# The first layer of a four-layer transformer kernel with another order of its pieces, written out as a table

## The chip, the cores and the metric

The kernel runs on one core of a Trainium2 chip. A core has five engines with instruction streams of their own, which meet only at semaphores: TensorE (PE, matrix products and transposes through the array), VectorE (DVE), ScalarE (ACT), GpSimd (POOL) and SyncE (SP, which only issues transfers here). The metric is the device time of one execution in microseconds, the median of several runs.

## The reference

Four layers, each a cross attention over 77 context rows per batch and then a feed-forward part. `x` has 4 x 512 = 2048 rows of 128 numbers. Only the first layer is touched:

```python
x = x + _L0_xattn_ref(_layernorm(x, axis=-1), ctx_1024, ctx_1024, mask_1x1xSxS2_fk1, ...)
x = x + _L0_ffn_ref(_layernorm(x, axis=-1), L0_ffn_gate_w, L0_ffn_w_up, L0_ffn_w_down, L0_ffn_expert_bias)
...
# _L0_xattn_ref, 16 heads of 8
q = _split_heads(query @ Wq + bq)
k = _split_heads(key @ Wk + bk)
v = _split_heads(value @ Wv + bv)
scores = jnp.einsum('bhqd,bhkd->bhqk', q, k) * scale
scores = scores + mask * -1000000000.0
attn = jax.nn.softmax(scores, axis=-1)
x = jnp.einsum('bhqk,bhkd->bhqd', attn, v)
return x.transpose(0, 2, 1, 3).reshape(...) @ Wo + bo
...
# _L0_ffn_ref, 8 experts, the best 2 for each row
scores = jax.nn.sigmoid(xf @ gate_w.T)
_, sel = jax.lax.top_k(scores + expert_bias, TOP_K)
# for each expert: (square(relu((xf * weight) @ wu.T))) @ wd.T, added up
```

## The kernel before

The 2048 rows are 16 tiles of 128. Work is cut into pieces such as `("S", 0, 3, 1)`, in the text S.0.3.1: kind S, layer 0, tile 3, second half of the heads. `make_plan` writes one list of pieces, the plan. Each engine's program walks that list and emits, for each piece, the instructions it has in it; so one list sets the order on all five engines, and the engines run apart from it only where no semaphore holds them.

The kinds of the first layer, with the line of their instructions in the profile of before:

- ln.q.0.g.0 to 7: the row normalisation of query group g, in steps (statistics L1385 and L1402 on DVE, step 2 on ACT L1889 and L1892, then L1406, L1410, L1415, and the scaled rows in steps 6 and 7, L1429, on DVE). ln.r is the same for the rows that go to the experts.
- xt: these rows turned by PE (L1073), and copied out by ACT (L1917). wq: the query projection (PE L1083), copied out half by DVE (L1323) and half by ACT (L1929), with the bias. The query groups are tiles 0, 1 to 3, 4 to 7, 8 to 11 and 12 to 15, and S of a tile waits for its group's wq.
- a0.n: the keys of batch n spread over heads (DVE L1344, four multiplications). vbd.n: the values likewise, on POOL (L2102, 2 instructions); vw0.n.q: turned by PE (L1023) and copied by ACT (L1852). xb: a bias on POOL (L2123).
- S: scores of a tile and 8 heads (PE L1095, 2 products recorded as 4). max: their maxima (DVE L1453). exp: the exponentials, 8 instructions on ACT (L1939). T.0.i.q: the probabilities turned by PE (L1118), in three parts q. copy.0.i.q: T copied out of its bank, by ACT (L1974) for q = 0 and 1 and by DVE (L1331) for q = 2. O: probabilities times values, and the sums (PE L1134, L1138). div: DVE L1495, L1499. Wo: PE L1151. add: DVE L1511. stat: DVE L1375.
- route.0.g.k and weigh: the choice of two experts for row group g and the place of each row in its expert's list, many short DVE instructions (L1521 to L1610) with PE products at k = 0 (L1163) and k = 9 (L1172 to L1176). send.0.i.c: an indirect DMA by POOL (L2143) that puts tile i's rows in place; 32 of them in the layer, in bursts of 8, 8, 6, 6 and 4.
- half, prod (PE L1037) and even, fold: work on the keys of layer 1, laid between.

Banks of the product memory bind the pieces: PE writes T with q = 0 and 2 to bank 4, and T with q = 1, xt and wq to bank 5, and a bank has to be copied out before its next writer. S of one half of the heads has banks 0 and 1, of the other 2 and 3, and they are free after that half's exp.

```python
bank_t = {p: 5 - (p[0] == "T" and p[3] != 1) for p in plan if p[0] == "wq" or p[0] == "T" and p[1] == 0 or
          p[0] == "xt" and p[2] == 0}
```

The expert blocks (X, U, H, D) start when all rows are sent, in `first`. Before, the plan of layer 0 came from rules: `first_order` for a tile's pieces, side lists that `tick` lets in after a given number of pieces, and `finish` for what is left at the end.

Of the kernel before, what the change touches and what calls it, by code (L numbers as in the profile page):

```python
# [166 lines left out]
def make_plan():  # L167
# [150 lines left out]
    def attention(L):  # L318
        for s in range(NT):
# [3 lines left out]
            for w in first_order(s) if L == 0 else order(L, s):  # L323
                if w is None:
                    drain(f"before{asked_of(L, s + (L > 0))}")
# [2 lines left out]
                tick(0 if w[0] in ("T", "exp") and L == 0 else 0 if s == NT - 1 else 1 + (L == 3) + (L > 0 and s == NT - 2))
# [12 lines left out]
    def finish(L):  # L341
# [38 lines left out]
        if L == 0:  # L380
            choice, rest = upto(("route", 0, 2, 6), rest)
            now(("T", 0, z, 0), ("O", 0, z - 1), ("copy", 0, z, 0), ("div", z - 1), ("T", 0, z, 1), ("T", 0, z, 2),
                ("copy", 0, z, 1), ("copy", 0, z, 2), ("Wo", z - 1))
            add(z - 1)
            now(*choice, ("O", 0, z), *rest[:1], *norm("r", 3, 1, 2), ("div", z), ("Wo", z), *rest[1:], *late, *norm("r", 3, 3, 4, 5, 6, 7))
# [1962 lines left out]
```

## Time and profile before

| | |
|---|---|
| median of 3 runs | 869.96 us (867.56 to 871.63) |
| profiled execution, its own time | 869.81 us |
| its span, first to last instruction | 868.5 us |
| from the span's start to the first expert block's input | about 192 us |
| instructions | 16687 |

The time of the profiled execution is 1.3 us above its span. A row of a timeline reads: start in us, duration in us, engine, line, operation, output <- input, sizes, how often, and in brackets how long the engine was idle before it and what ended that. In the view of waits a row says which engine and line waited for which, the total, how often, and the longest. "remote" is a releaser that the profile does not know.

### The profile page before, as it was taken

What the parts mean: (1) busy time and instruction counts of PE and PEld (TensorE: products, weight loads), DVE (VectorE), ACT (ScalarE), POOL (GpSimd) and SP (SyncE); (2) the same over time, 40 slices, a digit from 0 to 9 for tenths busy, and PEclk for the clock granted to TensorE, in tenths of its full rate; (3) what the DMA queues carried; (4) which work ended last, traced back from release to release, by engine and by line L of the source; (5) the groups of instructions that cost most, each with busy time, mean ns of one, the idle gap of its engine ahead of it and who ended that gap; (6) DMA issues with size and microseconds to landing.
All of it is one profiled execution on the core that took longest, in us unless ns stands there. A gap on an engine that the chain in (4) does not pass through costs nothing.

```text
span 868.5 us, 16687 instructions
## 1 busy us (share of the span) xinstructions
PE 734.1 (85%) x5129; PEld 600.7 (69%) x5129; DVE 536.2 (62%) x1879; ACT 507.5 (58%) x1720; POOL 289.9 (33%) x346
## 2 busy tenths in 40 slices
PE   3888875768778898898999899989999998877597
PEld 1566654647765577776996678878778875666597
DVE  3667844646655788764545897775232046886575
ACT  2677754246545898764565555667553348773375
POOL 0420033244561344453351444432000013253355
PEclk9799998688999999999999999999999999997599
DMA  8765995213315220001215870000000050000121
GB/s 275 261 206 185 302 215 150 69 44 88 82 56 190 71 73 5 11 14 41 76 45 161 207 190 1 1 2 1 1 1 1 1 188 7 2 16 14 48 73 48
DMA packets 37735, 74.21 MB, mean 85 GB/s; under 512 B 7360, under 2 KB 26944, under 8 KB 33680
## 3 DMA queue, kind: packets, MB, share of 16 engines
q1 hardware_dynamic: 32304, 62.97, 25.1%
q0 software_dynamic: 4768, 9.91, 3.4%
q8 instruction: 43, 0.70, 0.4%
q14 instruction: 44, 0.36, 0.1%
q10 hardware_dynamic: 576, 0.27, 0.1%
HBM read 63.03 MB, written 37.67 MB: 116 GB/s over the span
## 4 chain that ended last, share of the span: by engine, by line
PE 54%; DVE 16%; ACT 9%; issue 9%; POOL 7%; another core or an unknown queue 3%; DMA 1%; SPq 0%; POOLq 0%; DVEq 0%; ACTq 0%
PE bank L1250 10%; PE bank L1142 7%; PE bank L1212 5%; PE bank L1104 5%; PE bank L1222 5%; PE bank L1118 4%; PE bank L1050 3%; DVE s_xn L1429 3%; POOL xs_L L2143 3%; POOL out L2150 3%; PE bank L1095 2%; ACT s_S L1960 2%; PE bank L1202 2%; ACT s_S L1939 2%
## 5 line engine op out<-in xcount | busy, mean ns | idle before, releaser
L2115 POOL TENSOR_TENSOR s_S<-s_S,s_inv 128x462 f32<-128x462 f32 (+2 forms) x123 | 100.6, 835 | 139.2 <-DVE s_inv L1484 137.6
L1118 PEld LDWEIGHTS bank<-s_ident,s_S 128*128 128x128 f32 (+2 forms) x560 | 69.4, 145 | 74.6 <-issue 33.3
L1118 PE MATMUL bank<-s_ident,s_S 128*128 128x128 f32 (+2 forms) x560 | 91.3, 285 | 26.8 <-POOL s_S L2115 11.0
L1974 ACT ACTIVATE s_PT<-bank 128x512 f32<-128x512 f32 (+2 forms) x160 | 80.7, 507 | 53.7 <-PE bank L1118 41.6
L1104 PE MATMUL bank<-s_A,s_xTq 128*128 128x462 f32 (+2 forms) x256 | 104.6, 505 | 4.6 <-ACT s_S L1960 1.7
L1142 PE MATMUL bank<-s_VW,s_PT 128*128 128x128 f32 (+2 forms) x800 | 101.8, 284 | 0.0
L2143 POOL DMA_INDIRECT xs_L<-s_xn,s_sli x64 | 62.3, 974 | 112.5 <-DVE s_sli L1586 71.9
L1142 PEld LDWEIGHTS bank<-s_VW,s_PT 128*128 128x128 f32 (+2 forms) x800 | 97.9, 200 | 0.0
L1939 ACT ACTIVATE s_S<-bank,s_peak 128x77 f32<-128x77 f32 x256 | 59.2, 362 | 13.2 <-DVE s_peak L1453 13.1
L2016 ACT ACTIVATE s_hT<-bank,s_b1T 128x128 f32<-128x128 f32 x184 | 52.4, 370 | 22.0 <-issue 9.0
L1960 ACT ACTIVATE s_S<-bank,s_peak 128x77 f32<-128x77 f32 x192 | 60.8, 353 | 3.5 <-DVE s_peak L1470 3.4
L1212 PE MATMUL bank<-s_xeT,s_hs 128*128 128x128 f32 x360 | 55.0, 294 | 6.2 <-ACT s_xeT L1996 5.9
L2150 POOL DMA_INDIRECT ys_L<-s_yb,s_yi x43 | 41.3, 960 | 53.7 <-DVE s_yb L1703 25.5
L1948 ACT ACTIVATE s_S<-s_S 128x462 f32<-128x462 f32 (+1 forms) x64 | 35.6, 558 | 35.6 <-DVE s_S L1467 29.0
L1212 PEld LDWEIGHTS bank<-s_xeT,s_hs 128*128 128x128 f32 x360 | 48.8, 206 | 8.3 <-ACT s_xeT L1996 7.1
L1470 DVE TENSOR_REDUCE s_peak<-bank 128x6 f32<-128x462 f32 (+1 forms) x80 | 41.4, 526 | 15.2 <-PE bank L1118 10.7
L1050 PE MATMUL bank<-s_ctxT,s_GM 128*128 128x308 f32 x160 | 45.9, 441 | 4.9 <-DVE s_GM L1353 3.5
L1250 PE MATMUL bank<-s_fh,s_hh 128*128 128x512 f32 x128 | 50.0, 391 | 0.0
L1250 PE MATMUL bank<-s_fl,s_hh 128*128 128x512 f32 x128 | 49.8, 389 | 0.0
L1250 PE MATMUL bank<-s_fh,s_hl 128*128 128x512 f32 x128 | 49.8, 389 | 0.0
L1095 PE MATMUL bank<-s_A,s_XQ 128*128 128x308 f32 x128 | 44.4, 474 | 6.2 <-DVE s_A L1344 3.0
L1222 PE MATMUL bank<-s_moe,s_hT 128*128 x368 | 48.5, 276 | 1.2 <-ACT s_hT L2016 1.2
(233 smaller groups left out, 1638.8 us busy)
## 6 DMA issues: line engine op xcount, KB each, us to landing
xs_L<-xs_L SPq DMA_DIRECT2D x24, 1122.0 KB, 33.2
s_xe<-xs_L SPq DMA_DIRECT2D x85, 66.0 KB
s_moe<-in_L_w SPq DMA_DIRECT2D x2, 2048.0 KB, 10.6
s_moe<-in_L_w SPq DMA_DIRECT2D x8, 512.0 KB, 7.0
s_yb<-ys_L SPq DMA_DIRECT2D x12, 256.0 KB, 3.4
s_A<-in_keys SPq DMA_DIRECT2D x4, 616.0 KB, 6.6
s_arena<-in_L_w SPq DMA_DIRECT2D x2, 1024.0 KB, 12.4
s_arena<-in_L_h SPq DMA_DIRECT2D x2, 1024.0 KB, 9.1
```

What stands on the lines that cost most here:

```text
L1050: mm(bank[b][:, 0:BK], GM[:, slot, m:m + P], ctxT, start=True, stop=True).then_inc(fold_sum.up(L, v, h), 1)
L1104: mm(bank[b][:, 0:(h1 - h0) * KEYS], xTq_of(L, n)[:, i % 4, :], A[:, n, h0 * KEYS:h1 * KEYS], start=True, stop=True).then_inc(scores.up(L, ...
L1118: w = turn(bank[b][0:m, P * (t - t0):P * (t - t0) + P], S[s][:, P * t:P * t + m], ident)
L1142: w = mm(bank[b][:, 0:P], PT[k][0:m, t, :], VW[0:m, n, t, :], start=t == 0, stop=t == nt - 1)
L1212: w = mm(bank[b][:, P * t:P * t + P], wu[j % 3][:, P * t:P * t + P], xeT[q], start=True, stop=True)
L1222: w = mm(bank[b][:, 0:P], hT[q][:, P * t:P * t + P], down_w[L][:, bass.ds(expert[j] * hid + P * t, P)], start=t == 0, stop=t == hid // P - 1)
L1250: w = mm(bank[b], wt[:, c:c + P], ac[src][:, kk, :], start=n == 1, stop=n == 12)
L1939: w = a(S[s][:, o:o + KEYS], bank[2 * k + h // 4][:, c:c + KEYS], ACT.Exp, bias=peak[s][:, 8 * k + h:8 * k + h + 1])
L1960: w = a(S[s][:, h * KEYS:h * KEYS + KEYS], src[:, o:o + KEYS], ACT.Exp, bias=peak[s][:, h:h + 1], accum_out=total[s][:, h:h + 1])
L1974: w = a(flat(PT[k][:, full[0]:full[-1] + 1, :]), b[:, P * (full[0] - t0):P * (full[-1] - t0) + P], ACT.Copy)
L2115: p.tensor_tensor(val, val, rep(inv[s][:, h0:h1], KEYS, 2), ALU.mult).then_inc(normed.up(L, i, k), 1)
L2143: p.indirect_dma_start(xs[L], bass.IndirectOffsetOnAxis(ap=sli[:, c, i:i + 1], axis=0), xn[:, i, :], None).then_inc(sent.up(L, i, c), 16)
```

## The change

The pieces of layer 0, from the first normalised rows to the end of the schedule of the expert blocks, are taken from a table in place of the rules. Both plans hold the same 2287 pieces. The orders of POOL and SP come out the same; PE, DVE and ACT have theirs changed in many places by a few positions. A few pieces of layers 1 to 3 move by one position as well (a back transfer, a load), because side lists of layer 0 no longer exist; on no engine does that change the order of instructions.

```diff
+FIRST_LAYER = """
+    ln.q.0.0.0 ln.q.0.0.1 ln.q.0.0.2 ln.q.0.0.3 ln.q.0.0.4 ln.q.0.0.5 ln.q.0.0.6 ln.q.0.0.7 ln.q.0.1.0 ln.q.0.1.1
+        ln.q.0.1.2 xt.q.0.0 ln.q.0.1.3 ln.q.0.1.4 wq.0
+    S.0.0.0 ln.q.0.1.5 a0.0 ln.q.0.1.6 xt.q.0.1 xb.1
+    S.0.0.1 max.0.0.0 ln.q.0.1.7 ln.q.0.2.0 exp.0.0.0 max.0.0.1 spare wq.1 ln.q.0.2.1 T.0.0.0 vbd.0 xb.0 vw0.0.0
...
+    S.0.5.1 max.0.5.1 T.0.4.1 T.0.4.2 copy.0.4.1 copy.0.4.2 Wo.3 exp.0.5.1 add.0.3 vw0.2.2 a0.3 wq.3 stat.0.3
...
+def ordered(table):
+
+    return [tuple(int(x) if x.isdigit() else x for x in w.split(".")) for w in table.split()]
...
-    def first_order(s):
...
-        if L == 0:
-            choice, rest = upto(("route", 0, 2, 6), rest)
...
-    put("a0", 0)
-    near = [p for p in before(0, 1) if not isinstance(p, int)]
-    for piece in (("S", 0, 0, 0), *near[:1], ("max", 0, 0, 0), ("exp", 0, 0, 0), ("S", 0, 0, 1), *near[1:7],
-                  ("max", 0, 0, 1), *near[7:]):
+    for piece in ordered(FIRST_LAYER):
         put(*piece)
-    woven(values(0), [])
-    side("values", values(1) + values(2) + values(3) + [("load", "L1w"), ("tok",), ("clear", 1), ("cast",)])
-    put("spare")
-    put("clear", 0)
-    attention(0)
-    put("load", "L1v")
     experts(0)
```

The lines of the changed kernel stand 8 below those of before (L1939 is L1947 there). First place, ACT at the start of the program. Before, from exp.0.0.0 (the first L1939) to exp.0.0.1 (the second):

```order
L1939 ACTIVATE s_S_178<-bank,s_peak_78 128x77 x8
L1889 ACTIVATE s_nvq_94<-s_bag_q,s_eps 128x3
L1892 ACTIVATE s_nvq_95<-s_nvq_94 128x3
L1917 ACTIVATE s_xq<-bank 128x384
L1929 ACTIVATE s_XQ_174<-bank,s_bcol 32x384 x2
L1852 ACTIVATE s_V_168<-bank 128x96
L1852 ACTIVATE s_V_168<-bank 128x64
L1852 ACTIVATE s_V_168<-bank 128x32
L1852 ACTIVATE s_V_168<-bank 128x96
L1852 ACTIVATE s_V_168<-bank 128x32
L1852 ACTIVATE s_V_168<-bank 128x64
L1939 ACTIVATE s_S_178<-bank,s_peak_78 128x77 x8
```

and in the change, from the normalisation of tiles 1 to 3 to exp.0.0.1:

```order
L1897 ACTIVATE s_nvq_94<-s_bag_q,s_eps 128x3
L1900 ACTIVATE s_nvq_95<-s_nvq_94 128x3
L1925 ACTIVATE s_xq<-bank 128x128
L1937 ACTIVATE s_XQ_174<-bank,s_bcol 32x128 x2
L1925 ACTIVATE s_xq<-bank 128x384
L1947 ACTIVATE s_S_178<-bank,s_peak_78 128x77 x8
L1937 ACTIVATE s_XQ_174<-bank,s_bcol 32x384 x2
L1860 ACTIVATE s_V_168<-bank 128x96
L1860 ACTIVATE s_V_168<-bank 128x64
L1947 ACTIVATE s_S_178<-bank,s_peak_78 128x77 x8
```

The normalisation step of tiles 1 to 3 (L1889 and L1892 with 128x3) went from behind the first exponentials to ahead of all of them, xt.q.0.1 (L1917 with 128x384) went ahead of exp.0.0.0, and exp.0.0.1, which came behind all the L1852 of vw0.0, now stands between the first and the second of them. On DVE the first steps of that normalisation (L1385 with x3, L1402, L1406, L1410) stand ahead of wq.0 (L1323) in the change, where before they came behind a0.0; a0.1 went from ahead of max.0.1.0 to behind it.

Second place, DVE around wq.3 (L1323 with 32x512, in the change L1331), from max.0.5.0 to max.0.6.0. Before:

```order
L1453 TENSOR_REDUCE s_peak_80<-bank 128x8
L1495 RECIPROCAL s_yb_143<-bank 128x128
L1499 TENSOR_TENSOR s_yb_144<-bank,s_yb_143 128x128
L1323 TENSOR_SCALAR s_XQ_174<-bank,s_bcol 32x512 x2
L1453 TENSOR_REDUCE s_peak_80<-bank 128x8
L1331 COPY s_PT_181<-bank 128x256
L1511 TENSOR_TENSOR s_x<-bank,s_x 128x128
L1344 TENSOR_TENSOR s_A<-s_GM,s_hfour 32x308 x4
L1375 BN_STATS s_bst_r<-s_x 128x6
L1402 BN_AGGR s_bag_r<-s_bst_r 128x2 x4
L1453 TENSOR_REDUCE s_peak_78<-bank 128x8
```

and in the change:

```order
L1461 TENSOR_REDUCE s_peak_80<-bank 128x8
L1503 RECIPROCAL s_yb_143<-bank 128x128
L1507 TENSOR_TENSOR s_yb_144<-bank,s_yb_143 128x128
L1461 TENSOR_REDUCE s_peak_80<-bank 128x8
L1339 COPY s_PT_181<-bank 128x256
L1519 TENSOR_TENSOR s_x<-bank,s_x 128x128
L1352 TENSOR_TENSOR s_A<-s_GM,s_hfour 32x308 x4
L1331 TENSOR_SCALAR s_XQ_174<-bank,s_bcol 32x512 x2
L1383 BN_STATS s_bst_r<-s_x 128x6
L1410 BN_AGGR s_bag_r<-s_bst_r 128x2 x4
L1461 TENSOR_REDUCE s_peak_78<-bank 128x8
```

wq.3 went from ahead of max.0.5.1, copy.0.4.2, add.0.3 and a0.3 to behind all four. wq.4 goes in the same way from ahead of max.0.9.1 and copy.0.8.2 to behind them.

Third place, PE at the end of the layer, from Wo.15 (L1151, in the change L1159) on. Before:

```order
L1151 MATMUL bank<-s_wo,s_yb_144 128x128
L1073 MATMUL bank<-s_ident,s_xn 128x128 x3
L1163 MATMUL bank<-s_gT,s_xTr_164 128x8 x3
L1037 MATMUL bank<-s_wqT,s_wk 128x128 x16
L1172 MATMUL bank<-s_asg,s_tri 128x24
L1174 MATMUL bank<-s_asg,s_ones 128x16
L1174 MATMUL bank<-s_asg,s_ones 128x8
L1176 MATMUL bank<-s_base_124,s_ones 128x24
L1050 MATMUL bank<-s_ctxT,s_GM 128x308 x2
```

and in the change:

```order
L1159 MATMUL bank<-s_wo,s_yb_144 128x128
L1045 MATMUL bank<-s_wqT,s_wk 128x128 x8
L1081 MATMUL bank<-s_ident,s_xn 128x128 x3
L1171 MATMUL bank<-s_gT,s_xTr_164 128x8 x3
L1045 MATMUL bank<-s_wqT,s_wk 128x128 x8
L1180 MATMUL bank<-s_asg,s_tri 128x24
L1182 MATMUL bank<-s_asg,s_ones 128x16
L1182 MATMUL bank<-s_asg,s_ones 128x8
L1184 MATMUL bank<-s_base_124,s_ones 128x24
L1058 MATMUL bank<-s_ctxT,s_GM 128x308 x4
```

Half of the products L1037 for layer 1's keys (half and prod of the first eight heads) went ahead of xt.r.0.3 (L1073), the other half stayed behind route.0.3.0 (L1163).

## Rows read from the trace of the kernel before

**Rows 1.** The page's head and its first part: span, then busy time by engine.

```profile
span 868.5 us, 16687 instructions
...
PE 734.1 (85%) x5129; PEld 600.7 (69%) x5129; DVE 536.2 (62%) x1879; ACT 507.5 (58%) x1720; POOL 289.9 (33%) x346
```

**Rows 2.** Windows: PE, PEld, DVE, ACT, POOL busy (instructions), PEclk, DMA share, GB/s.

```profile
36.00:107.00 71.00, 60.42 (x719) 45.85 (x721) 54.94 (x173) 53.87 (x209) 8.55 (x7) 1.00 0.71 229
107.00:120.00 13.00, 8.43 (x104) 5.91 (x93) 3.76 (x8) 6.00 (x23) 7.86 (x8) 0.95 0.99 203
...
138.00:151.00 13.00, 6.01 (x69) 3.85 (x67) 2.26 (x6) 4.66 (x18) 7.68 (x8) 0.80 0.38 126
```

**Rows 3.** Timeline of the start, DVE, PE, POOL and ACT one after another.

```profile
12.58 1.92 DVE L1344 TENSOR_TENSOR s_A<-s_GM,s_hfour 32x308 f32<-32x308 f32 x4
14.54 0.68 DVE L1385 BATCH_NORM_STATS2 s_bst_q<-s_x 128x6 f32<-128x128 f32 x3
...
21.42 0.79 DVE L1453 TENSOR_REDUCE s_peak<-bank 128x8 f32<-128x616 f32 x1
...
26.62 3.65 DVE L1344 TENSOR_TENSOR s_A<-s_GM,s_hfour 32x308 f32<-32x308 f32 x4
...
14.76 4.45 PE L1095 MATMUL bank<-s_A,s_XQ 128*128 128x308 f32 x8 [2.96 <-DVE s_A L1344]
22.52 0.55 PE L1073 MATMUL bank<-s_ident,s_xn 128*128 128x128 f32 x3 [3.32 <-DVE s_xn L1429]
23.65 1.65 PE L1083 MATMUL bank<-s_xq,s_wqT 128*128 128x384 f32 x2 [0.58 <-ACT s_xq L1917]
...
35.66 0.53 PE L1095 MATMUL bank<-s_A,s_XQ 128*128 128x308 f32 x1 [0.87 <-ACT s_S L1939]
...
23.57 2.40 POOL L2102 TENSOR_TENSOR s_Vbd<-s_GM,s_hmask 128x616 f32<-128x616 f32 x2
...
26.35 2.62 POOL L2102 TENSOR_TENSOR s_Vbd<-s_GM,s_hmask 128x616 f32<-128x616 f32 x2
...
30.20 1.84 ACT L1939 ACTIVATE s_S<-bank,s_peak 128x77 f32<-128x77 f32 x8
...
33.79 1.82 ACT L1939 ACTIVATE s_S<-bank,s_peak 128x77 f32<-128x77 f32 x8
```

**Rows 4.** Waits of PE from 36 to 107 us.

```profile
PE bank L1118 <- DVE s_PT L1331: 3.0, 2, 1.5
...
PE bank L1095 <- ACT s_XQ L1929: 1.8, 1, 1.8
...
PE bank L1118 <- ACT s_xq L1917: 1.1, 1, 1.1
```

**Rows 5.** Timeline around wq.3: DVE, then PE, then ACT.

```profile
66.43 1.52 DVE L1323 TENSOR_SCALAR s_XQ<-bank,s_bcol 32x512 f32<-32x512 f32 x2 [3.62 <-PE bank L1083]
...
68.70 0.41 DVE L1331 COPY s_PT<-bank 128x256 f32<-128x256 f32 x1
...
69.17 0.66 PE L1118 MATMUL bank<-s_ident,s_S 128*128 128x128 f32 x4 [1.52 <-DVE s_PT L1331]
...
68.82 1.41 ACT L1939 ACTIVATE s_S<-bank,s_peak 128x77 f32<-128x77 f32 x6 [1.02 <-DVE s_peak L1453]
```

**Rows 6.** Timeline, end of POOL's second burst of sends and DVE behind it.

```profile
147.52 0.96 POOL L2143 DMA_INDIRECT xs_L<-s_xn,s_sli  x1 [0.30 <-issue]
...
150.18 0.96 DVE L1495 RECIPROCAL s_yb<-bank 128x128 f32<-128x128 f32 x1 [10.01 <-remote]
```

**Rows 7.** Timeline of PE behind the last tile.

```profile
165.84 0.90 PE L1073 MATMUL bank<-s_ident,s_xn 128*128 128x128 f32 x3 [2.73 <-DVE s_xn L1429]
...
168.70 3.79 PE L1037 MATMUL bank<-s_wqT,s_wk 64*128 64x128 f32 x32
172.42 0.62 PE L1172 MATMUL bank<-s_asg,s_tri 128*128 128x24 f32 x2
```

More of the change, by code:

```diff
@@ L97 @@
+"""
+def ordered(table):
+    return [tuple(int(x) if x.isdigit() else x for x in w.split(".")) for w in table.split()]
 class Signal:
@@ L322, in attention @@
                     side(f"before{g}", before(L, g))
[L323 removed]
+            for w in order(L, s):
                 if w is None:
[L325 removed]
+                    drain(f"before{asked_of(L, s + 1)}")
                     continue
                 put(*w)
[L328 removed]
+                tick(0 if s == NT - 1 else 1 + (L == 3) + (L > 0 and s == NT - 2))
                 if w[0] == "add":
@@ L378, in keyed @@
             return part
-        if L == 0:
-            choice, rest = upto(("route", 0, 2, 6), rest)
[L382 to L385, printed above, removed]
-            add(z)
-            now(("xt", "r", 0, 3), *steps("route", 3, 0), ("sigm", 0, 3))
-            now(*norm("r", 4, 1, 2), *keyed(5), *steps("route", 3, 1, 2, 3, 4, 5, 6, 9), *steps("weigh", 3, 0, 1, 2),
-                *steps("route", 3, 7, 10, 11, 12), *sends(0, 3), *norm("r", 4, 3, 4, 5, 6, 7), *keyed(3),
-                ("xt", "r", 0, 4), *steps("route", 4, 0), ("sigm", 0, 4), *keyed(3),
-                *steps("route", 4, 1, 2, 3, 4, 5, 6), ("sched", 0, 0), *steps("route", 4, 9), *steps("weigh", 4, 0, 1, 2),
-                *keyed(2), *steps("route", 4, 10, 11, 12), *sends(0, 4), *(("sched", 0, st) for st in (1, 2)),
-                *keyed(len(key)), *(("sched", 0, st) for st in range(3, 7)))
-            return
-        elif L == 1:
+        if L == 1:
             gate, rest = upto(("route", 1, 2, 0), rest)
@@ L464, in finish @@
             *keyed(len(key)), *(("sched", L, st) for st in range(3, 7)))
-    def woven(a, b):
-        a, b = ([p for p in q if not isinstance(p, int)] for q in (a, b))
-        n = 0
-        for k, piece in enumerate(a):
-            put(*piece)
-            while n < len(b) * (k + 1) // len(a):
-                put(*b[n])
-                n += 1
-        for piece in b[n:]:
-            put(*piece)
     def values_and_rows(L):
@@ L506, in make_plan @@
     put("v0")
-    for piece in before(0, 0):
-        if not isinstance(piece, int):
-            put(*piece)
-    def values(n):
-        out = [("a0", n), 5] if n else []
-        out += [("vbd", n), *[("xb", 0)] * (n == 0), 6]
-        for q in range(len(spans(0))):
-            out += [("vw0", n, q), 3]
-        return out
-    put("a0", 0)
-    near = [p for p in before(0, 1) if not isinstance(p, int)]
-    for piece in (("S", 0, 0, 0), *near[:1], ("max", 0, 0, 0), ("exp", 0, 0, 0), ("S", 0, 0, 1), *near[1:7],
-                  ("max", 0, 0, 1), *near[7:]):
-        put(*piece)
-    woven(values(0), [])
-    side("values", values(1) + values(2) + values(3) + [("load", "L1w"), ("tok",), ("clear", 1), ("cast",)])
-    put("spare")
-    put("clear", 0)
-    attention(0)
-    put("load", "L1v")
+    for piece in ordered(FIRST_LAYER):
+        put(*piece)
     experts(0)
```

80 lines of the change are left out of this document (62 added, 18 removed).

## Prediction

> **What bounds the kernel now.** The page comes first: PE is busy for 734.1 of 868.5 us and no other engine for more than 536.2 [rows 1]. The layer that changes ends at about 192 us; what follows depends on it only through its end, since no load or clear that the rest needs is still on its way then. So a microsecond won before the first expert block should be one at the end. Next the view by windows, to see how much there is to win. From 36 to 107 us PE is busy for 60.42 of 71 us [rows 2]: the loop over tiles leaves 10.6 us of PE idle, and no order can win more than that there, since the work is the same. Two later stretches are of another kind: from 107 to 120 us PE works 8.43 of 13 us and from 138 to 151 us 6.01 of 13 [rows 2], and in both POOL issues eight sends back to back. Third, the timeline of the start: PE has next to nothing to do until 14.76, and then waits 3.32 us for the normalised rows at 22.52 [rows 3]. Fourth, PE's waits from 36 to 107 us, each put down to the piece it belongs to [rows 4].
>
> **The start (term A).** Before, ACT does exp.0.0.1 at 30.20, although the maxima for it stood at 22.21 (21.42 and 0.79) [rows 3]. It queues behind wq.1 and all of vw0.0, and these behind the normalisation of tiles 1 to 3. I follow the new order with the old durations. The steps of that normalisation that go ahead of wq.0 (0.68 us of statistics [rows 3], plus some short ones, partly in DVE's idle time) make wq.0 and a0.0 later by about 1.1 us, so S.0.0.0 starts near 15.9 and not 14.76. It takes half of 4.45 us: end 18.1, its maxima end near 19.0, the last rows near 19.4, and xt.q.0.1 goes at about 19.5 where it went at 22.52: 3.0 earlier. S.0.0.1 (2.2 us) now stands between xt.q.0.1 and wq.1, so wq.1 starts near 22.1 and not 23.65: 1.5 earlier. POOL's vbd.0, which needs the same rows, comes 3 us earlier than 23.57 and is off the path. ACT then does vw0.0.0 and at once exp.0.0.1, near 25.7 and not 30.20: 4.5 earlier. S.0.1.0 follows at 26.8, exp.0.1.0 at 29.8 where it stood at 33.79: 4.0 earlier. S.0.2.0, which waits for that exp, stands at 35.66 and would come near 31.7. On DVE a0.1 (3.65 us before, beside POOL's vbd.1 from 26.35 to 28.97; the same piece alone took 1.92 [rows 3]) moves behind max.0.1.0 and holds max.0.1.1, which therefore gains only some 2.5 us. Between 2.5 and 4.0 I take **3.5 us**, near the upper end, since S.0.2.0 waits for the exp and not for max.0.1.1.
>
> **Query group 2 (term B).** T.0.2.1 waits 1.1 us for ACT's copy of xt.q.0.2 out of bank 5, and S.0.4.0 waits 1.8 us for wq.2 [rows 4]. In the new order ACT does that copy ahead of exp.0.3.0, and PE does T.0.3.0 and O.0.2 ahead of S.0.4.0. Both waits are 2.9 us; nothing is won below 0, and exp.0.4.0 cannot start sooner than its scores. I take about half, **1.5 us**.
>
> **wq.3 and wq.4 (term C).** DVE stands idle 3.62 us for wq.3's product and then takes 1.52 us for it, while max.0.5.1 and copy.0.4.2 are queued behind; the copy ends at 69.11, PE's T.0.5.0 has waited 1.52 us for it, and ACT's exp.0.5.1 starts at 68.82 [rows 5]. With the two ahead of wq.3, max.0.5.1 can go as soon as DVE is free near 63, so that exp is ready some 4 us earlier. PE wins at least its wait of 1.5, and a part of the wait ahead of the product. I take 2.0. The same pattern stands at wq.4: the two waits of PE for DVE's copy are 3.0 us in sum [rows 4], so 1.5 us is there; DVE's wq.4 moves behind and delays max.0.10.0 instead, so I take 1.2. Term C is **3.2 us**, between 0 and 5.
>
> **What the new order loses (term D).** exp.0.12.1 now stands behind copy.0.12.0 on ACT, and S.0.13.1 needs its banks. An exp takes 1.84 us [rows 3]; O.0.11 on PE covers a part. Between 0 and 1.84 I take **1.0 us** lost. On the layer's other places I found moves of one or two short instructions and cost them at nothing: the waits of DVE and ACT cover them.
>
> **The end of the layer (term E).** PE waits 2.73 us ahead of xt.r.0.3, then does the products for layer 1's keys in 3.79 us, and the counting product route.0.3.9 comes only at 172.42, at their very end [rows 7]. Half of them, 1.9 us, go into the 2.73 us of waiting and fit there. The count can then start up to 1.9 us earlier, but its operands come from DVE, and what they allow is in no row here: between 0 and 1.9 I take half, 1.0 us. Also O.0.14 goes ahead of T.0.15.0, which brings its div and O.0.15 earlier by less than 1 us. Between 0 and 2 I take **1.3 us** won.
>
> **Sum.** 3.5 + 1.5 + 3.2 - 1.0 + 1.3 = 8.5 us. The profiled execution took 869.81 us, so 861.3; it lies 0.15 us from the median of the runs shown, so no further correction. I round off half a microsecond for waits that reappear elsewhere in a loop in which DVE and ACT are busy 54.94 and 53.87 of 71 us [rows 2] and forecast 862 us. With every term at its lower bound, 2.5 + 0 + 0 - 1.84 + 0 = 0.7 us are won, with every one at its upper, 4.0 + 2.9 + 5 - 0 + 2 = 13.9 us.
>
> **What the bursts of sends do.** At 150.18 DVE has waited 10.01 us for a sum of O.0.13 whose product ended long before, for a releaser that the profile calls remote; POOL's last send of that burst ended at 148.48 (147.52 and 0.96) [rows 6]. PE lost 4.6 us of the first stretch and 7.0 us of the second. I read it as signals of PE that arrive only behind POOL's burst. The Trainium skill says otherwise, in "SBUF — State Buffer", section "Who interferes with whom": PE and ACT never wait on anyone, and only DVE and GpSimd can block each other, for one instruction. By that rule the 10.01 us would have nothing to do with the sends, and no order of the sends against the tiles could cost anything. The rows do not agree with it, but they don't show the mechanism either. It changes nothing in the sum, which prices the bursts at no change; by the page rival 3 below would be worth nothing.
>
> **Rivals.**
> 1. The forecast: terms A to E hold roughly. Chance 0.60, time 857 to 866, centre 862.
> 2. Only the start is won. The loop over tiles is as tight as its engines allow, each wait that is taken from one place comes back in the next, and 3.5 - 1.0 = 2.5 is left, or 3.8 with E: 866.0 to 867.3. For it speaks that DVE and ACT are three quarters busy there; against it that ACT and DVE waited themselves where PE did [rows 5]. Chance 0.22.
> 3. The held signals decide, and the kernel is slower. DVE's route.0.0.12 comes about 1 us earlier against the tile work, and S.0.11.1, Wo.9 and O.0.10 then fall inside the first burst. If what PE's followers wait for is held to the end of every burst, then eight sends at 0.30 + 0.96 = 1.26 us [rows 6] cost 10.1 us: 5.5 more than the first stretch's 4.6, and 3.1 more than the second's 7.0. The third burst, six sends or 7.6 us, would hold the gates of route.0.3.0, at a price that I put between 0 and half of it; with 3.5 the whole is 12.1 against the 8.5 won, and the time 873.4. It decides from 8.5 us of such losses on, so it needs more than the first burst. For it speaks the wait of 10.01 us, against it that the first burst cost half as much as the second with the same eight sends. Chance 0.12, of which half ends slower by more than 0.5% (by a third burst held for longer) and the rest within it.
> 4. The new order wins more: the first or second burst falls where nobody waits for PE, so that a part of its 4.6 or 7.0 us comes on top of the sum. With 4 us of these the time is 857.3, with the upper bounds of terms A to C too some 5 less: 850 to 857. Chance 0.06.
> That the change doesn't do what it says can be left out: the lists of instructions per engine show it.
>
> **How the numbers follow.** About 0.5% (4.3 us) is what a measurement of this kernel can tell from no change: below 865.6 counts as faster, above 874.3 as slower. From the cases: case 1 almost whole (0.58), case 4 (0.06) and a small part of case 2 (0.04) are faster: 0.68. Case 2's rest and most of case 3 are the same: 0.26. Slower: 0.06. The range reaches from 855 to 869, which leaves out the ends of cases 3 and 4 and the tail of case 1; case 1 alone is 857 to 866.
>
> **What the profile of the changed kernel would show.** A: exp.0.0.1 at ACT near 26 and S.0.2.0 near 32. B: no wait of PE for ACT's s_xq, no wait of PE ahead of S.0.4.0. C: DVE's wq.3 with max.0.5.1 ahead of it and no wait near 3.6 us; PE's waits for DVE's s_PT from the start of the loop to the first send close to nothing. D: a wait of PE L1103 for ACT near tile 13. E: PE's wait ahead of xt.r.0.3 under 1 us, with the products for the keys on both sides of it. Rival 3 would show as "remote" waits at the bursts while PE idles more than 4.6 and 7.0 us there. The prediction would be wrong if the waits for the bursts changed by more than 4 us, or if the loop's PE idle time stayed near 10 us.

## The result, and the profile after

The changed kernel took 846.28 us (median; 844.19 to 846.91), the kernel before 870.8 us in the same comparison: ratio 0.9719, 95% interval 0.9692 to 0.9746. That is 24.5 us won, where 8.5 were forecast and 855 was the lower end of the range. The page's head and its first part, for the changed kernel:

```profile
span 844.9 us, 16691 instructions
...
PE 725.1 (86%) x5129; PEld 594.8 (70%) x5129; DVE 534.2 (63%) x1879; ACT 506.0 (60%) x1720; POOL 289.7 (34%) x346
```

DVE, ACT and POOL are busy for at most 2 us less than before [rows 1]. PE is busy 9 us less, and idle 15 us less (844.9 - 725.1 = 119.8; before 868.5 - 734.1 = 134.4).

The windows that answer to [rows 2]: the 71 us ahead of the first burst of sends, the 13 us of the first burst and the 13 us of the second, both of which now start 15 to 18 us earlier.

```profile
22.00:93.00 71.00, 65.97 (x770) 50.66 (x769) 61.08 (x188) 60.31 (x238) 12.37 (x12) 1.00 0.87 268
92.00:105.00 13.00, 9.26 (x121) 6.68 (x110) 5.04 (x12) 5.67 (x22) 7.85 (x8) 0.87 1.00 212
...
120.00:133.00 13.00, 6.07 (x68) 3.71 (x66) 2.44 (x9) 4.58 (x19) 7.66 (x8) 0.85 0.97 260
```

In the first row PE is idle 5 us and not 10.6, but the row begins ahead of the loop over the tiles. From S.0.2.0 to the first send, in the change and then in the kernel before:

```profile
29.54:92.40 62.86, 59.29 (x717) 46.15 (x721) 55.21 (x175) 53.53 (x211) 8.54 (x7) 1.00 0.85 257
```

```profile
35.66:107.36 71.70, 61.12 (x732) 46.51 (x736) 55.13 (x173) 54.35 (x210) 8.55 (x8) 1.00 0.72 229
```

The loop is 8.8 us shorter, and PE is idle 3.6 us in it and not 10.6. The two bursts cost it 3.7 and 6.9 us of idle time, where they cost 4.6 and 7.0. So the loop was tightened, and the bursts cost nearly what they did.

The timeline of the start, PE and then ACT and DVE (start, duration, engine, line, operation, and in brackets the idle time ahead of it and what ended it):

```profile
15.47 2.39 PE L1103 MATMUL bank<-s_A,s_XQ 128*128 128x308 f32 x4 [3.04 <-DVE s_A L1352]
19.01 0.90 PE L1081 MATMUL bank<-s_ident,s_xn 128*128 128x128 f32 x3 [1.15 <-DVE s_xn L1437]
25.37 1.20 PE L1103 MATMUL bank<-s_A,s_XQ 128*128 128x308 f32 x4
29.54 1.30 PE L1103 MATMUL bank<-s_A,s_XQ 128*128 128x308 f32 x4 [0.35 <-ACT s_S L1947]
...
24.85 1.84 ACT L1947 ACTIVATE s_S<-bank,s_peak 128x77 f32<-128x77 f32 x8
27.65 1.83 ACT L1947 ACTIVATE s_S<-bank,s_peak 128x77 f32<-128x77 f32 x8
...
27.33 1.92 DVE L1352 TENSOR_TENSOR s_A<-s_GM,s_hfour 32x308 f32<-32x308 f32 x4
```

Against [rows 3]: xt.q.0.1 goes at 19.01 (22.52), exp.0.0.1 at 24.85 (30.20), exp.0.1.0 at 27.65 (33.79), S.0.2.0 at 29.54 (35.66). That is 6.1 us at S.0.2.0, where term A said 3.5. a0.1 takes 1.92 us and not 3.65; it no longer runs beside POOL's vbd.1, which ends at 25.23.

Around wq.3, DVE and then PE, as in [rows 5]:

```profile
55.15 0.80 DVE L1461 TENSOR_REDUCE s_peak<-bank 128x8 f32<-128x616 f32 x1 [1.19 <-PE bank L1103]
55.87 0.41 DVE L1339 COPY s_PT<-bank 128x256 f32<-128x256 f32 x1
56.20 0.28 DVE L1519 TENSOR_TENSOR s_x<-bank,s_x 128x128 f32<-128x128 f32 x1
56.40 1.91 DVE L1352 TENSOR_TENSOR s_A<-s_GM,s_hfour 32x308 f32<-32x308 f32 x4
58.34 1.52 DVE L1331 TENSOR_SCALAR s_XQ<-bank,s_bcol 32x512 f32<-32x512 f32 x2
...
58.23 0.60 PE L1126 MATMUL bank<-s_ident,s_S 128*128 128x128 f32 x4
```

DVE's 3.62 us of waiting ahead of wq.3 and PE's 1.52 us ahead of T.0.5.0 are both gone, and T.0.5.0 stands 10.9 us earlier. PE's waits in the 71 us (total, times, longest) have one row left of those in [rows 4]:

```profile
PE bank L1031 <- ACT s_V L1860: 1.8, 3, 0.7
PE bank L1159 <- DVE s_yb L1507: 1.0, 2, 0.7
...
PE bank L1126 <- DVE s_PT L1339: 0.2, 1, 0.2
```

Near tile 13, where term D expects it, PE waits for ACT ahead of S.0.13.1:

```profile
111.78 1.30 PE L1103 MATMUL bank<-s_A,s_XQ 128*128 128x308 f32 x4 [0.97 <-ACT s_S L1947]
```

How much earlier each checkpoint stands on PE or POOL than before (starts in the two traces): S.0.2.0 6.1, S.0.5.1 8.0 (61.89 and 53.91), O.0.4 11.0 (69.76, 58.77), O.0.8 14.05 (99.62, 85.57), O.0.13 18.2 (139.70, 121.52), last send of the layer 18.3 (188.34, 170.04), DVE's first copy of the keyside products of layer 1 21.1 (263.35, 242.25), and from 300 us on 23.5. So 5.3 of 23.6 us arise behind the layer, where no engine's order changed.

Two stretches show how. The first is at the last returns of the expert blocks. In the kernel before, around 260 us, DVE, then POOL, then PE's products that the copy takes up:

```profile
263.35 1.29 DVE L1353 COPY s_GM<-bank 128x512 f32<-128x512 f32 x2 [3.72 <-remote]
...
258.65 0.96 POOL L2150 DMA_INDIRECT ys_L<-s_yb,s_yi  x1 [0.30 <-issue]
259.92 0.96 POOL L2150 DMA_INDIRECT ys_L<-s_yb,s_yi  x1 [0.30 <-issue]
261.18 0.96 POOL L2150 DMA_INDIRECT ys_L<-s_yb,s_yi  x1 [0.30 <-issue]
...
259.16 2.06 PE L1037 MATMUL bank<-s_wo,s_wv 64*128 64x128 f32 x32
```

and the same in the changed kernel:

```profile
242.25 1.28 DVE L1361 COPY s_GM<-bank 128x512 f32<-128x512 f32 x2
...
239.77 0.96 POOL L2158 DMA_INDIRECT ys_L<-s_yb,s_yi  x1 [0.30 <-issue]
242.35 0.95 POOL L2158 DMA_INDIRECT ys_L<-s_yb,s_yi  x1 [1.63 <-DVE s_yb L1707]
...
240.50 2.06 PE L1045 MATMUL bank<-s_wo,s_wv 64*128 64x128 f32 x32
```

Before, the last five returns stood back to back, and DVE's copy started 1.2 us behind the last one's end and 4.2 us behind the start of the products. Now there is a gap of 1.63 us in the returns, and the copy starts 1.75 us behind the start of the products. So a lead of 18.7 us became one of 21.1 here.

The second stretch is TensorE's speed. From 192 to 300 us its granted clock was 0.91 of full speed before, and 1.00 in the change. The same products of layer 1, before and then in the change:

```profile
297.16 1.75 PE L1104 MATMUL bank<-s_A,s_xTq 128*128 128x462 f32 x2
298.70 0.85 PE L1118 MATMUL bank<-s_ident,s_S 128*128 128x128 f32 x3
```

```profile
274.84 0.94 PE L1112 MATMUL bank<-s_A,s_xTq 128*128 128x462 f32 x2
275.62 0.49 PE L1126 MATMUL bank<-s_ident,s_S 128*128 128x128 f32 x3
```

They took nearly twice as long before. The lead is 22.3 us ahead of these two rows and 23.4 behind them (299.34, 275.95). What made the speed fall there was not tried.

### The profile page after: what moved, and what is told of

Read it like the earlier page. It is cut to its first block, busy times and chain, and to the rows that moved or that the text cites. A ratio compares the mean times of both kernels' runs of the same rounds, so it can differ in the third digit from the quotient of the medians.

```text
span 844.9 us, 16691 instructions
## 1 busy us (share of the span) xinstructions
PE 725.1 (86%) x5129; PEld 594.8 (70%) x5129; DVE 534.2 (63%) x1879; ACT 506.0 (60%) x1720; POOL 289.7 (34%) x346
## 4 chain that ended last, share of the span: by engine, by line
PE 55%; DVE 16%; issue 9%; ACT 9%; POOL 6%; DMA 2%; another core or an unknown queue 2%; SPq 0%; POOLq 0%; DVEq 0%; ACTq 0%
PE bank L1258 10%; PE bank L1150 7%; PE bank L1220 5%; PE bank L1230 5%; PE bank L1112 5%; PE bank L1126 4%; DVE s_xn L1437 3%; POOL out L2158 3%; PE bank L1103 3%; POOL xs_L L2151 2%; ACT s_S L1968 2%; PE bank L1210 2%; PE bank L1058 2%; PE bank L1081 2%
## 5 line engine op out<-in xcount | busy, mean ns | idle before, releaser
L1947 ACT ACTIVATE s_S<-bank,s_peak 128x77 f32<-128x77 f32 x256 | 59.0, 374 | 7.5 <-DVE s_peak L1461 7.4
L1478 DVE TENSOR_REDUCE s_peak<-bank 128x6 f32<-128x462 f32 (+1 forms) x80 | 41.3, 526 | 14.4 <-PE bank L1126 10.1
L1112 PEld LDWEIGHTS bank<-s_A,s_xTq 128*128 128x128 f32 x256 | 40.4, 195 | 12.7 <-issue 5.5
```

Of the source, the lines that this page charges most:

```text
L1112: mm(bank[b][:, 0:(h1 - h0) * KEYS], xTq_of(L, n)[:, i % 4, :], A[:, n, h0 * KEYS:h1 * KEYS], start=True, stop=True).then_inc(scores.up(L, ...
```

## Two kinds of comparisons

The experiments are six comparisons, each with its own runs of the kernel before. In four of them that kernel took 833 to 836 us, in two 870, as on record. The traces say what differs: in the 870 us kind, signals of TensorE and other engines arrive late behind back-to-back indirect DMAs of GpSimd (waits for "remote" of up to 10.5 us); in the traces of the other kind no wait up to 200 us is put down to "remote". I call the kinds held (H) and free (U). The kind can't be chosen, so each kernel is compared with the kernel before of its own comparison. What sets the kind is open: each comparison ran on a chip of its own (the record has numbers 0, 11, 14 and 15 for U, 1 and 3 for H), and no chip came twice, so it may belong to the chip or to something else that differed.

| run | kernel | kind | us | before | ratio (95%) |
|---|---|---|---|---|---|
| e1 | new order up to S.0.2.0 only | U | 830.7 | 832.9 | 0.9947 (0.9917 to 0.9978) |
| e10 | same | U | 826.9 | 833.2 | 0.9915 (0.9883 to 0.9947) |
| e13 | same | U | 827.0 | 833.1 | 0.9940 (0.9911 to 0.9969) |
| e2 | new order but for the start | U | 825.6 | 832.9 | 0.9906 (0.9868 to 0.9944) |
| e3 | before, start filled with transposes | U | 834.7 | 832.9 | 1.0008 (0.9974 to 1.0042) |
| e4 | new order up to S.0.10.1 | U | 820.7 | 832.9 | 0.9821 (0.9783 to 0.9860) |
| e17 | same | H | 854.4 | 870.1 | 0.9791 (0.9753 to 0.9829) |
| e5 | the change | H | 848.3 | 869.8 | 0.9746 (0.9711 to 0.9781) |
| e12 | the change | U | 826.4 | 833.1 | 0.9923 (0.9894 to 0.9952) |
| e6 | before | H | 870.1 | 869.8 | one run |
| e7 | before, all sends of layer 0 spaced | H | 869.8 | 869.8 | 0.9981 (0.9941 to 1.0020) |
| e8 | before, wq.3 and wq.4 moved | H | 866.7 | 869.8 | 0.9945 (0.9897 to 0.9993) |
| e9 | the change, first two bursts spaced | U | 824.0 | 833.2 | 0.9890 (0.9836 to 0.9945) |
| e11 | same | U | 825.3 | 833.1 | 0.9900 (0.9851 to 0.9949) |
| e15 | same | U | 821.8 | 836.0 | 0.9860 (0.9799 to 0.9921) |
| e14 | before, first two bursts spaced | U | 833.9 | 833.1 | 1.0013 (0.9984 to 1.0042) |
| e16 | same | U | 836.3 | 836.0 | 1.0018 (0.9982 to 1.0054) |
| e18 | order of e4, first two bursts spaced | H | 835.0 | 870.1 | 0.9623 (0.9586 to 0.9661) |

## The experiments

**The order in parts.** The first layer's order is a table in the changed kernel, so a part of the change is a table with one order up to a piece and the other from there on. e1, e10 and e13, of which only FIRST_LAYER differs from the change, go over to the old order at S.0.2.0:

```diff
-    S.0.2.0 T.0.1.0 copy.0.1.0 exp.0.2.0 ln.q.0.2.7 O.0.0 div.0 ...
+    S.0.2.0 T.0.1.0 O.0.0 copy.0.1.0 exp.0.2.0 div.0 ...
```

> The new order up to S.0.2.0 and the order of before from there. Theory 1 (the wins of the new order add up, and each lasts to the end): S.0.2.0 starts 6.1 us earlier than before (29.54 and 35.66 in the two profiles), and so does the first expert block, so the kernel takes about 864.7 us. Theory 2 (a large part of the 24.5 us comes from chance effects after the layer, where TensorE's granted clock and the waits behind the sends fall otherwise): the first expert block comes 6 us earlier, but the end comes anywhere from 2 to 11 us earlier. Theory 3 (what the start wins is taken back in the loop over the tiles by ACT and DVE): 868 us or more.

> The new order up to S.0.2.0 alone once more, in search of a comparison where signals are held. The lead of 6 us at S.0.2.0 had fallen to 5.2 us at S.0.9.0 in the run without held signals. Theory 1 (a lead lasts): 864 us where before takes 870, and the layer's last send 5 to 6 us earlier. Theory 2 (a lead below the wait that comes next is lost in the bursts and in the clock behind them, as that of wq.3 and wq.4 was between 131 and 150 us): the lead at the second burst's end is under 2 us, and the time within 2 us of before.

> The new order up to S.0.2.0. Without held signals it led by 5.2 to 6 us behind S.0.2.0 and won 2 to 6 us in the end. Where signals are held: 864 us if a lead goes through the bursts, 868 or more if the second burst takes it back, as it took that of wq.3 and wq.4.

All three came out U: 2.2, 6.3 and 6.1 us won by the medians. S.0.2.0 stood at 30.00 in e13 and at 35.21 in e14, which has the old start in the same comparison. In e10 and e13 the lead of the start reached the end. e1 is the same kernel as e10, and its trace shows where its lead went. Both wait 1.66 us (e10 1.65) for T.0.13.0, and behind that wait PE runs at different speeds, in e1 and then in e10:

```profile
120.84 1.58 PE L1146 MATMUL bank<-s_PT,s_hk 128*32 128x128 f32 x24
```

```profile
119.94 0.87 PE L1146 MATMUL bank<-s_PT,s_hk 128*32 128x128 f32 x24
```

The second burst then starts at 129.33 in e1 and at 125.25 in e10. So two traces of one kernel can differ by 4 us here. That 864 us holds in kind H was not measured. e2 has the start of before and the new order behind it:

> The order of before up to S.0.2.0 and the new order from there. Theory 1: the changed kernel's 846.3 us plus the 6.1 us of the start, 852.4 us, and together with the kernel that has the new start alone the two parts sum to the whole. Theory 2: the first expert block comes 6 us later than in the changed kernel, the end anywhere from 2 to 11 us later. Theory 3 (the start isn't worth its 6.1 us at the end): 850 us or less.

It won 7.3 us, as much as the whole change in this kind (e12: 6.7). So theory 1, that the parts sum, is wrong for kind U: 6 and 7 don't make 6.7 (the wait for a load, read below, is the likely reason). e4 and e17 stop at tile 10:

> The new order up to S.0.10.1 and the order of before from there, with the old places of exp.0.12.1 and of the tail. Theory 1 (the sum of the steps in the two traces): S.0.10.1 starts 14 us earlier than before, and the end comes 14 us earlier, 856.8 us. If the order from tile 10 on is what brings the 4.3 us between S.0.10.1 and the last send of the layer, the last send stands 14 us earlier and not 18.3. Rival: these 4.3 us come from the first burst of sends falling at another place against the tiles, which this kernel has too; then the last send stands 17 us or more earlier.

> The new order up to S.0.10.1 and the old one from there, once more. Without held signals: 12 us under before, and so some 5 us under the whole change, if the order from tile 10 on costs that much there; 7 us under before if the difference was between calls. With held signals: 852 to 857 us if the bursts cost as in the order before, under 850 if they cost as in the change.

In kind U this won 12.2 us, more than the whole change; in kind H 15.6, less than the whole change. What stands from tile 10 on therefore costs some 5 us in kind U. In kind H it brings 6 us against e5 and 9 against the comparison on record, but these are different comparisons, and the intervals of e17 and e5 meet. In the traces, the last send of e17 stands 3.4 us behind that of the change (173.48, 170.04).

**TensorE's speed at the start.** From vw0.0 on, the changed kernel's products at the start take half of the time of the same products before (S.0.0.1, ahead of them, still took 2.26 us). PE before (the second row is S.0.1.0), and then in the change:

```profile
26.03 1.12 PE L1023 MATMUL bank<-s_ident,s_Vbd 128*128 128x128 f32 x4 [0.73 <-POOL s_Vbd L2102]
...
29.71 2.26 PE L1095 MATMUL bank<-s_A,s_XQ 128*128 128x308 f32 x4
```

```profile
23.65 0.60 PE L1031 MATMUL bank<-s_ident,s_Vbd 128*128 128x128 f32 x4
...
25.37 1.20 PE L1103 MATMUL bank<-s_A,s_XQ 128*128 128x308 f32 x4
```

Before, they come behind PE's wait of 3.32 us [rows 3]; in the change PE waits 1.15 us there. This goes with the order: S.0.1.0 took 1.20 us in all twelve traces with the new start, and 1.94 to 2.26 in all eight with the old one. e3 fills the old wait with work:

```diff
                     w.then_inc(scores.up(0, i, k), 1)
+                    if (i, k) == (0, 1):
+                        for _ in range(18):
+                            turn(bank[OUT][:, 0:P], ident, ident)
                     continue
```

> The kernel before, with 18 transposes of the identity, whose results nobody reads, put on TensorE behind S.0.0.1, in the 3.3 us in which it waited for xt.q.0.1. No piece moves. If half of the start's 6.1 us is the clock (granted 0.50 from 24 to 33 us before, 1.00 in the change), the granted clock stays at 1.00 from 21 to 33 us, S.0.1.0 takes 1.2 us and not 2.26, and S.0.2.0 starts 1.5 to 3 us earlier. If only the order counts, because the weighted values and ACT set the pace there, S.0.2.0 starts within 0.5 us of 35.66.

The transposes took 2.68 us from 18.95 on. The first products of vw0.0, behind a wait of 1.47 us, then took 0.66 us and not 1.12, but those behind the next wait, of 0.46 us, took 1.11 again, and S.0.1.0 took 2.26 us. S.0.2.0 came only 0.5 us earlier, at 35.16, and two traces without the transposes have it there too (35.15 in e7, 35.21 in e14). So this run could not decide.

> The kernel before once more, for its trace beside those of these runs. If the held signals are the difference between 870.8 and 832.9 us, this trace has the first 107 us as in the profile of before, and every microsecond between them arises at and behind the bursts of sends and in layer 0's expert blocks, whose three sends stand back to back; if the two chips differ in general, the difference grows evenly over the span.

e6 keeps within about 1 us of the profile on record all the way, so a trace of kind H repeats. Against the profile on record, the kernel before in kind U (e14's trace, with its first two bursts spaced, which costs nothing there) is within 1.1 us up to the first burst. It is 14.4 us earlier at the first product of the expert blocks (193.23, 178.84), and 31.4 us at the rows of layer 1 (276.20, 244.82): 14 of the 36 us between these two traces arise at the sends and 17 in layer 0's expert blocks. So the two kinds differ there and not in general. e6 also warns of the clock column. From 24 to 33 us, in the profile on record and then in e6 (the last three columns are granted clock, DMA share, GB/s):

```profile
24.00:33.00 9.00, 7.30 (x21) 4.50 (x21) 6.71 (x15) 4.14 (x17) 4.97 (x5) 0.50 0.87 342
```

```profile
24.00:33.00 9.00, 7.65 (x21) 4.73 (x22) 6.45 (x15) 4.24 (x17) 4.85 (x5) 1.00 0.86 340
```

Granted were 0.50 and 1.00, and S.0.1.0 took 2.26 us in both and S.0.2.0 started at 35.66 and 35.54. How fast TensorE is must be read from the durations here.

> The changed kernel once more. In the comparison on record both kernels had waits behind the bursts of sends that the profile calls remote; in the four runs above no signal of TensorE came late and the kernel before took 832.9 us, not 870.8. Theory 1 (the change is worth its 24.5 us only where the sends hold signals, because it also shifts the bursts): where no signal is late it takes about 12 us less than before, near 820.7 us, the time of the kernel with the new order up to S.0.10.1. Theory 2 (the order from tile 10 on is worth 4 us of its own): near 816 us. Where signals are late again, both give 24 us less than before.

> The changed kernel itself. Where no signal is held: 824 us where before takes 833, 9 us less, if the order alone is what the prediction's terms priced; 809 us if the 24.5 us don't depend on held signals. Where signals are held: 847 us, as twice before.

The change wins 21.5 us in kind H and 6.7 in kind U. The expectation that the order from tile 10 on is worth 4 us of its own fell.

**wq.3 and wq.4 alone (term C).** The order of before, with two pieces moved:

```diff
-    ... vw0.2.2 wq.3 max.0.5.1 copy.0.4.2 Wo.3 exp.0.5.1 add.0.3 a0.3 ...
+    ... vw0.2.2 max.0.5.1 copy.0.4.2 Wo.3 exp.0.5.1 add.0.3 a0.3 wq.3 ...
-    ... route.0.0.3 wq.4 max.0.9.1 route.0.0.4 load.L1k copy.0.8.2 route.0.0.5 ...
+    ... route.0.0.3 max.0.9.1 route.0.0.4 load.L1k copy.0.8.2 route.0.0.5 wq.4 ...
```

> The order of before with two pieces moved on all engines: wq.3 behind a0.3 and wq.4 behind route.0.0.5, as in the new order. Theory 1 (term C of the prediction): DVE's wait of 3.6 us ahead of wq.3 is gone and TensorE wins 2 to 3 us at T.0.5.0 and 1 to 2 at T.0.9.0, together 3 to 5 us at the end. Rival: wq.3's half on DVE now delays S.0.8.0's queries or the next maxima, and less than 1 us is left.

O.0.8 stood 3.9 us earlier (95.69 for 99.62), and 3.3 of it was there already at wq.4's product (91.71 for 95.03): up to there theory 1 holds, in size too. But at 151 us nothing of it was left in this trace. Windows of e8 from 130 to 140 us, and of the kernel before:

```profile
130.00:140.00 10.00, 10.00 (x58) 8.04 (x51) 4.47 (x17) 4.46 (x18) 1.07 (x2) 0.52 0.63 189
```

```profile
130.00:140.00 10.00, 7.88 (x98) 6.25 (x101) 8.64 (x33) 7.06 (x28) 1.03 (x2) 1.00 1.00 223
```

e8's TensorE was busy all of the 10 us and did 58 products where before did 98: it ran at its lower level, 1.2 GHz, behind a wait of 1.66 us at 128.22. The second burst started at 138.63, before at 138.66, and its end is what the rest waits for. Thirteen traces have this wait ahead of T.0.13.0 (1.65 to 1.87 us). Behind it the products ran at the lower level in e1, e3, e4, e8, e14 and e18 and at full speed in the other seven, and e1 and e10, e14 and e16, e4 and e17 are pairs of one kernel each. So it isn't shown that e8 lost its lead by its order. Its ten runs took 858.6 to 871.6 us, four of them under 862, and the profiled one was among the slow ones with 870.7. In the end e8 was 3 us faster by the medians, with an interval that reaches to 0.6 us. What decides between the two speeds is open. The seven traces with the new order from tile 10 on don't have the wait.

**The bursts.** If signals wait for a gap in GpSimd's indirect DMAs, gaps must free them. e7 puts six short memsets, each waiting for the one before, behind each send of layer 0:

```diff
                                      None).then_inc(sent.up(L, i, c), 16)
+                for _ in range(6 if L == 0 else 0):
+                    if paced.n:
+                        pool.wait_ge(*paced.at(paced.n))
+                    p.memset(pad, 0.0).then_inc(paced.up(), 1)
```

> The kernel before, with six short memsets on GpSimd behind each send of layer 0, each waiting for the one before, so that two sends have about 1.5 us of other work between them. Where signals are held during a burst: they come through in the gaps, TensorE works through the first two bursts, and about 8 of the 11.6 us that it lost there come back, less some 2 to 4 us because the last sends of the layer stand later. Where no signal is held: only the later sends are left, 5 to 12 us slower.

The sends then stand 2.33 us apart and not 1.26. The window of the first burst in e7, where [rows 2] has 8.43 us and 104 products for the same 13 us:

```profile
107.00:120.00 13.00, 12.32 (x172) 10.07 (x176) 8.75 (x21) 11.02 (x44) 9.59 (x35) 1.00 0.99 234
```

PE works through it, in kind H. The kernel led by 14.4 us at xt.r.0.3 (151.41, before 165.84 [rows 7]), and paid it back with the last sends of the layer, which end what the expert blocks wait for: last send at 188.31, before at 188.34. So e9 and e14 space the first two bursts only (`L == 0 and i < 8`). The expectations, of all comparisons:

> The changed kernel, with the six short memsets behind each send of tiles 0 to 7, so behind the first two bursts only. Where signals are held (before near 870 us): the changed kernel's TensorE is idle 5 to 6 us at the first burst and 9 us at the second; in the spaced order without the change these two were nearly gone. Theory 1 (the rest of the layer is paced by this work): 8 to 12 us less than the changed kernel, some 836 us. Rival (behind the second burst the work is paced by something else, so the held wait only hides another): at most 3 us less. Where no signal is held: no difference to the changed kernel, since POOL has nothing else to do there.

> The changed kernel with memsets behind the sends of the first two bursts, once more. Where signals are held: without these two bursts the changed kernel wins 8 to 12 us, 836 to 840 us, if the end of the layer is paced by this work; 845 or more if something else takes their place. Where none is held: 824 us as in the run before.

> The changed kernel with memsets behind the sends of the first two bursts. Where signals are held: if the held waits of these bursts are on the path, 8 to 12 us under the changed kernel's 847, so 836 to 840 us; if something else takes their place, 845 us or more. Where none is held: 825 us again.

> The kernel before, with the memsets behind the sends of tiles 0 to 7 only. Where signals are held: the spaced kernel had a lead of 12.8 us at 150 us and lost it by spacing the last sends of the layer, which end later; with those left alone the lead should stay, 857 us. If it is the same 870 us as before, the lead is lost at the later bursts for another reason. Where none is held: within 2 us of before.

> The kernel before with the same memsets. Where signals are held: 857 us if the lead of 12.8 us that the spaced kernel had at 150 us stays; 866 or more if the later bursts, held as ever, take it. If the difference between this kernel and the changed one with the same memsets is 7 us, as without held signals, the first two bursts make the 16 us; if it is 20 us or more, the later ones do. Where none is held: 833 us again.

All five came out U, in spite of two labels: the memsets cost nothing there (1.0013 and 1.0018 for the kernel before). What they win in kind H was seen in one pair, on the order of e4:

> The same order with the memsets behind the sends of tiles 0 to 7. Without held signals: the same time as the kernel above, within 2 us. With held signals: 10 us or more under it if the first two bursts are on the path, and the best of all kernels there; within 3 us of it if the later bursts take the lead back.

835.0 us against e17's 854.4 in the same comparison: 19.4 us, the best kernel of kind H. Windows of the first two bursts in e17, and then of the longer, spaced ones in e18:

```profile
92.00:105.00 13.00, 9.63 (x120) 6.87 (x108) 4.20 (x8) 5.71 (x21) 7.86 (x8) 0.87 1.02 232
122.00:135.00 13.00, 5.76 (x69) 3.84 (x67) 2.14 (x6) 4.66 (x18) 7.68 (x8) 0.86 0.84 261
```

```profile
92.00:112.00 20.00, 17.25 (x216) 13.38 (x216) 13.93 (x50) 14.83 (x59) 15.37 (x56) 1.00 0.99 211
119.00:138.00 19.00, 12.95 (x197) 10.36 (x195) 13.04 (x57) 8.17 (x30) 15.08 (x55) 0.94 0.98 243
```

In e17 PE did 120 and 69 products in 13 us each; in e18 216 and 197 in 20 and 19, where e17 did 200 and 126 (from 92 and 122 us on). Its layer ended 11.2 us earlier (last send 162.28 and 173.48). Behind the layer the two traces move apart by another 11.7 us. 3.0 of these arise at the returns, as above: the lead is 11.7 at the products (243.09, 231.37) and 14.7 at DVE's copy (247.28, 232.59). The rest was not followed up.

**What the tail costs in kind U.** PE behind the last tile, in e12 (the change) and then in e4 (the old order from tile 10 on):

```profile
128.53 0.49 PE L1159 MATMUL bank<-s_wo,s_yb 128*128 128x128 f32 x2
140.38 2.08 PE L1045 MATMUL bank<-s_wqT,s_wk 64*128 64x128 f32 x16 [11.36 <-DMA s_wqT<-in_L_wqT]
142.39 0.90 PE L1081 MATMUL bank<-s_ident,s_xn 128*128 128x128 f32 x3
```

```profile
134.72 0.51 PE L1159 MATMUL bank<-s_wo,s_yb 128*128 128x128 f32 x2 [0.32 <-DVE s_yb L1507]
137.94 0.90 PE L1081 MATMUL bank<-s_ident,s_xn 128*128 128x128 f32 x3 [2.72 <-DVE s_xn L1437]
...
140.80 3.79 PE L1045 MATMUL bank<-s_wqT,s_wk 64*128 64x128 f32 x32
```

The change is 6.2 us ahead at Wo.15, and then waits 11.36 us for the weights of layer 1's keys, because half.1.1.0 stands ahead of xt.r.0.3. xt.r.0.3, route.0.3 and the sends queue behind it: it goes at 142.39, in e4 at 137.94. That is 4.45 us, and 5.2 at the last send (163.48, 158.26), against 5.7 between the medians of e4 and e12. No run moved these products alone, so the cause is read from the traces. The weights' load is issued behind clear.1 on SyncE's queue and landed there at 133 to 140 us in all five runs with the new tail in kind U (waits of 3.9, 5.0, 8.4, 10.8 and 11.4 us). In kind H PE comes to it at 145.19 and the load is there.

## Why the prediction was wrong

- **Sign:** right. The prediction's first step, that a microsecond ahead of the expert blocks is one at the end, was not: in kind H the lead was 18.3 us at the last send and 23.6 at the end. In kind U it came nearer to that: 10.9 and 7.8 us at the last send (e12 against e14 and e16), 8.1 and 8.5 at the end.
- **A, 3.5 us:** measured 6.1, over its upper bound of 4.0. The step that failed is "I follow the new order with the old durations". vw0.0's transposes (0.60 and 0.66 us for 1.12 and 1.11) and S.0.1.0 (1.20 for 2.26) are 2.0 us shorter together, where 2.6 us were missing. This is read from the two traces; no run separated it from the order.
- **B, 1.5 us:** measured 1.9 (6.1 at S.0.2.0, 8.0 at S.0.5.1). Both waits are gone.
- **C, 3.2 us:** 3.0 between S.0.5.1 and O.0.4, and 3.05 between O.0.4 and O.0.8, where wq.4 stands; 3.9 of this were shown as wq.3 and wq.4 alone in e8. The mechanism and size of the two moves were right. About 2 us are left, for which the other moves remain, of which the prediction said "cost them at nothing"; no run separated them.
- **D, 1.0 us lost:** the wait that it foresaw is there, 0.97 us ahead of S.0.13.1, and still the sign was wrong, since the order there also ends other waits. From O.0.8 to O.0.13 the lead grows by 4.1 us. In e17, with the old order there, it grows by only 1.4 (from 14.6 to 16.0). So the new order brings about 2.7 us, among them the wait of 1.66 us ahead of T.0.13.0, which is gone. The other 1.4 came with e17's order too.
- **E, 1.3 us won:** from O.0.13 to the last send 0.1 us in kind H. PE's wait ahead of xt.r.0.3 went from 2.73 to 1.54 us there. In kind U it has the wrong sign, -4.5 us (e12 against e4), and the step that failed is that half of the products "fit there", in the wait ahead of xt.r.0.3: I priced the products as work that fits into a wait, and not as an instruction that itself waits for a load. Every piece moved ahead brings its own waits with it.
- **The sum:** up to O.0.8, A + B + C was 8.2 and measured 14.05. That is the larger error in the layer: A and C were priced too small, A with durations that did not hold and C, as far as is known, for moves set at nothing. Behind the layer come 5.3 us that no term had.
- **The signals:** the reading that PE's signals arrive only behind POOL's burst was right in mechanism (e7, e18), and rival 3's price was not: the bursts cost 10.7 us of PE's idle time for 11.6. The prediction weighed against this a rule of the Trainium skill ("SBUF — State Buffer", section "Who interferes with whom"), that PE and ACT never wait on anyone. That section speaks of the ports of the SBUF, and the prediction stretched it to whatever a send might hold up. Stretched so it fails in kind H, where the spaced sends took the waits away; whether it holds for the ports, no run here tests.
- **The rivals:** the measured 846.3 us lies below all four. Rival 4 had the right direction, but its reason, that a burst falls where nobody waits, was worth 0.9 us. Its sum was off too: the upper bounds of A to C are 3.7 us above the terms, not some 5, so its case with 4 us of the bursts ends at 853.6 and not 850.
- **The range** took the profile on record for the only state of the machine. 862 us came from 8.5 us won; in kind U 6.7 us were won, but by other terms than those of the sum (14.5 us at O.0.8, 86.23 in e12 and 100.72 in e14, less what the wait for the load took). That the number fits there is luck.

What stays open: what sets the kind; how much of the 17 us that kind H loses in the expert blocks spacing the returns would give back; and the clock's part behind 300 us. The order of e4 with the spaced bursts ran in kind H alone; in kind U e4 without them was the best at 820.7 us.

## What to carry to other kernels

When a chain is shortened, don't re-use the old durations of its steps: ask for each what it ran beside and at which of its two speeds TensorE ran it, since both can change. A piece put ahead of others on an in-order engine must have its own operands there, loads too, at the earliest time at which the engine may now reach it; the profile of the slow kernel doesn't show that wait. Look at a second trace of the same kernel before explaining a stretch: here TensorE's speed behind one wait differed between traces of one kernel. And where an order is tuned on one machine, measure the parts of it on a second, since here the same tail cost 5 us on one and not on another.
